# Writing the layer norms' row-wise products and sums on GpSimd as four instructions of 256 columns

## The reference

```
mask = adjacency_matrix.astype(float32) + eye(n) > 0
for l in range(3):
    si = x @ attn_w[l, :d];  sj = x @ attn_w[l, d:]
    scores = leaky_relu(si[:, :, None] + sj[:, None, :] + attn_b[l], 0.2)
    attn = softmax(where(mask, scores, -inf))
    h = layernorm(x + attn @ x, g1[l], beta1[l])
    x = layernorm(h + gelu(h @ W1[l] + b1[l]) @ W2[l] + b2[l], g2[l], beta2[l])
# layernorm(x, gamma, beta) = (x - mu) * rsqrt(var + eps) * gamma + beta
```

## Time and profile before

| | us |
|---|---|
| median of 3 runs | 1895.09 |
| lowest, highest | 1894.74, 1895.41 |
| profiled execution, span | 1892.0 |
| PE busy | 1672.9 (88%) |
| DVE busy | 1513.0 (80%) |
| POOL busy | 1314.4 (69%) |
| ACT busy | 1120.7 (59%) |

### The profile page before, as it was taken

One profiled execution on the slowest core, in us unless ns is written; L12 is line 12 of the kernel. 1 busy time (PEld: TensorE's weight loads), 2 busy tenths in 40 slices (PEclk: granted clock), 3 DMA queues, 4 the chain that ended last, 5 costly groups with the idle time before them and its releaser, 6 DMA issues.

```text
span 1892.0 us, 40139 instructions
## 1 busy us (share of the span) xinstructions
PE 1672.9 (88%) x12032; PEld 1482.6 (78%) x12032; DVE 1513.0 (80%) x5366; ACT 1120.7 (59%) x2718; POOL 1314.4 (69%) x1690
## 2 busy tenths in 40 slices
PE   5999999965999999999899999999989898989895
PEld 4777777754888888888788888888878787878784
DVE  3888888877788778788887887887888888888873
ACT  3888888864556556556465565565554545554542
POOL 3355555534787787787777877877868787888786
PEclk8999999996999999999899999999999898999998
DMA  5233333323121121121211211211212122212101
GB/s 181 63 89 89 89 89 89 89 79 123 34 67 58 42 67 58 42 67 54 91 56 44 67 52 47 67 53 47 67 34 68 64 70 65 68 64 69 63 26 45
DMA packets 150477, 127.31 MB, mean 67 GB/s; under 512 B 14880, under 2 KB 143392, under 8 KB 150432
## 3 DMA queue, kind: packets, MB, share of 16 engines
q1 hardware_dynamic: 145024, 124.30, 21.4%
q10 hardware_dynamic: 5408, 2.50, 0.5%
HBM read 89.03 MB, written 37.75 MB: 67 GB/s over the span
## 4 chain that ended last, share of the span: by engine, by line
PE 24%; DVE 20%; POOL 19%; issue 11%; ACT 3%; POOLq 1%; DVEq 0%; ACTq 0%
PE ps L45 14%; PE ps L819 6%; POOL gnn_norm L154 5%; DVE gnn_junk L913 5%; PE ps L795 3%; DVE gnn_small L929 2%; POOL gnn_norm L742 2%; POOL gnn_h L746 2%; POOL xo L761 2%; POOL gnn_norm L757 2%; POOL inv L149 2%; DVE gnn_small L934 2%; DVE gnn_small L937 2%; DVE gnn_res L972 1%; DVE gnn_st L976 1%
## 5 line engine op out<-in xcount | busy, mean ns | idle before, releaser
L819 PE MATMUL ps<-gnn_w_hi,gnn_g_hi 128*128 128x256 f32 x1536 | 454.8, 296 | 41.7 <-DVE gnn_res L972 41.0
L819 PE MATMUL ps<-gnn_w_lo,gnn_g_hi 128*128 128x256 f32 x1536 | 445.7, 290 | 0.0
L819 PE MATMUL ps<-gnn_w_hi,gnn_g_lo 128*128 128x256 f32 x1536 | 444.9, 290 | 0.0
L141 POOL TENSOR_TENSOR fence_pool<-half_neg 128x1 f32<-128x1 f32 x304 | 64.1, 213 | 477.3 <-DVE gnn_mv L1063 169.0
L980 DVE TENSOR_TENSOR gnn_g_lo<-ps,gnn_g_hi 128x512 fp32r<-128x512 f32 x384 | 263.1, 685 | 135.3 <-ACT ps L893 135.2
L892 ACT ACTIVATE gnn_g_hi<-ps,b_cols 128x512 fp32r<-128x512 f32 x384 | 264.5, 689 | 179.4 <-PE ps L45 155.3
L819 PEld LDWEIGHTS ps<-gnn_w_hi,gnn_g_hi 128*128 128x128 f32 x1536 | 305.6, 199 | 47.5 <-DVE gnn_res L972 44.8
L45 PE MATMUL ps<-gnn_hT_hi,gnn_w_hi 128*128 128x512 f32 x768 | 333.4, 434 | 4.0 <-DVE gnn_g_lo L980 4.0
L869 ACT ACTIVATE gnn_e<-gnn_u,gnn_small 128x128 f32<-128x128 f32 x192 | 74.9, 390 | 400.3 <-DVE gnn_small L938 400.3
L819 PEld LDWEIGHTS ps<-gnn_w_lo,gnn_g_hi 128*128 128x128 f32 x1536 | 306.7, 200 | 1.9
L819 PEld LDWEIGHTS ps<-gnn_w_hi,gnn_g_lo 128*128 128x128 f32 x1536 | 305.8, 199 | 0.0
(11 more groups left out here) (116 smaller groups left out, 3925.2 us busy)
## 6 DMA issues: line engine op xcount, KB each, us to landing
hist<-xo SPq DMA_DIRECT2D x48, 512.0 KB, 3.3
x<-hist SPq DMA_DIRECT2D x48, 512.0 KB, 4.3
gmask<-mask_hist SPq DMA_DIRECT2D x48, 256.0 KB, 4.5
aw<-in_L_gnn_attn_w SPq DMA_DIRECT2D x48, 256.0 KB, 4.3
att_xq<-in_x SPq DMA_DIRECT2D x16, 512.0 KB, 4.8
att_xl<-in_x SPq DMA_DIRECT2D x16, 512.0 KB, 3.5
gnn_fin<-hist SPq DMA_DIRECT2D x16, 512.0 KB, 3.8
out<-gnn_fin SPq DMA_DIRECT2D x16, 512.0 KB, 2.8
```

Source lines behind the costliest of these rows:

```text
L141: e.tensor_tensor(fence_pool[:, n:n + 1], half_neg[:, 0:1], half_neg[:, 0:1], ALU.add)
L819: mm = e.matmul(FF2[j % 2], g[a][:, m, j * N:(j + 1) * N], V[b][:, m, :], start=(n == 0), stop=(n == len(terms) - 1))
```

## The change

Each of the five instructions of 128x1024 becomes four of 128x256, one for each graph; `row` gives one row and no longer repeats it. The semaphore is raised by the last of the four. Nothing else is written differently: waits, values and the order on all engines stay.

```
                 def row(l, n):
-                    return affine[:, bass.ds(l, 1), n, :].to_broadcast([P, GROUP, D])
+                    return affine[:, bass.ds(l, 1), n, :].rearrange("p o d -> p (o d)")
...
                     e.wait_ge(ln1, 6 * t1 + 5)
-                    e.tensor_tensor(norm[:], norm[:], row(l, 0), ALU.mult).then_inc(ln1, 1)
+                    for j in range(GROUP):
+                        ins = e.tensor_tensor(norm[:, j, :], norm[:, j, :], row(l, 0), ALU.mult)
+                    ins.then_inc(ln1, 1)
...
-                    e.tensor_tensor(h[:], norm[:], row(l, 1), ALU.add).then_inc(h_out, 1)
-
-                    e.tensor_tensor(hb[par1][:], norm[:], row(l, 2), ALU.add).then_inc(hb_out, 1)
+                    for j in range(GROUP):
+                        ins = e.tensor_tensor(h[:, j, :], norm[:, j, :], row(l, 1), ALU.add)
+                    ins.then_inc(h_out, 1)
+
+                    for j in range(GROUP):
+                        ins = e.tensor_tensor(hb[par1][:, j, :], norm[:, j, :], row(l, 2), ALU.add)
+                    ins.then_inc(hb_out, 1)
...
-                    e.tensor_tensor(norm[:], norm[:], row(l, 3), ALU.mult).then_inc(ln2, 1)
+                    for j in range(GROUP):
+                        ins = e.tensor_tensor(norm[:, j, :], norm[:, j, :], row(l, 3), ALU.mult)
+                    ins.then_inc(ln2, 1)
...
-                    e.tensor_tensor(xo[par][:], norm[:], row(l, 4), ALU.add).then_inc(x_out, 1)
+                    for j in range(GROUP):
+                        ins = e.tensor_tensor(xo[par][:, j, :], norm[:, j, :], row(l, 4), ALU.add)
+                    ins.then_inc(x_out, 1)
```

## The result

| | before | changed |
|---|---|---|
| median | 1894.57 us | 1899.27 us |
| lowest, highest (9 runs each) | 1892.05, 1895.41 | 1896.46, 1903.24 |
| profiled execution, span | 1892.0 | 1897.3 |
| POOL busy | 1314.4 | 1438.7 |

A forecast was written before the change was run, and what follows sets the result against it. POOL was taken to bound the first two layers. Steady steps +5, PE's clock +31, last layer +4, start and end +2.5 on 1892.0 gave 1934.5; with 3.1 for the median of the runs, 1937, range 1894 to 1966.

The forecast's parts named there:

- rival (1): PE's clock holds: then +11.5, 1907 us; chance 0.20, range 1895 to 1912.
- The signs named for being right: Groups 2.75 to 2.85; L939, L947 under 0.8; behind h 5.5 to 6 or 7 to 7.5; PE's stall 2 to 2.5.
- The ring and its bound: First two layers: POOL sets the 28.33 us steady step, 21.16 of it on POOL and 7.17 behind h.
- Four quarters: Each group of four costs POOL +0.40 us over one instruction; four groups count in a steady step, +1.60.
- rival (2): Quarters cost next to nothing, at most 0.1 to 0.2 a group: 1860 us; chance 0.12.
- What DVE gets back: Behind h, DVE's small instructions wait less: 7.17 becomes 5.59, -1.58 a step; their slipping between quarters adds +0.15.
- PE's clock: A 2.3 us stall before the transposes lowers the clock in 0.6 of 30 steps, 1.7 each: +31 us.
- PEclk at 9 in all slices: Sign of being wrong: granted PE clock at 9 in all the page's slices of the first two layers.
- The last layer: POOL never idle, a step of 31.85 for 31.52: +0.3 a step over 14 steps, +4 us.
- Start and end: The first and last norms run alone, six groups: +2.5 us.
- Rival (3): `probs_max` gets in before h's last quarter, holds POOL 0.66, clock always falls: +76, 1975 us; chance 0.10.
- Rival (4): DVE gains nothing, the 7.17 behind h stays: +53 to +60, 1955 us; chance 0.10.

The follow-up runs named there:

- the PSUM kernel: Kernel before, no group cut, rows of DVE's small tile placed in PSUM so its small instructions read at most one SBUF tensor: 1803.05 us, ratio 0.9523.
- keeping PE busy: Changed kernel plus twelve unused transposes of the identity on PE ahead of its wait for h: 1874.39 us, ratio 0.9909.
- three groups cut: Kernel before with only the three groups of `ln_attention` (product, h, hb) in quarters, `ln_ffn` whole: 1855.84 us, ratio 0.9803.
- changed, small rows in PSUM: Changed kernel, all five groups in quarters, with the rows of DVE's small tile in PSUM: 1932.75 us, ratio 1.0202.

## Why the prediction was right and wrong

The forecast was +42 and the measurement is +4.7. The step that failed is the account of POOL's and DVE's standing still for each other. The sum took DVE's small instructions as a cost to POOL (+0.15 a step) and put at nothing, without a reason, what POOL gets back in its own fronts; the runs showed 0.2 to 0.9 a step less there, so that the ring without a fall of the clock became shorter, and the last layer gained 9.5 us where +4 was forecast. The second step is one of size: 31 for the falls of the clock, of which some 22 came. The measured 1899 lies inside the stated range, but in the interval of rival (1), 1895 to 1912, whose mechanism, that the clock holds, did not happen: that number would be right by luck. The signs named for being right came in the steady steps: groups of 2.78 to 2.83, L939 at 0.80 and L947 at 0.16, stretches of 5.58 and 7.07, stalls of 1.94 and 2.27.

**The ring and its bound** were read rightly. POOL sets a steady step, the ends of L929 and L937 with POOL's instructions were the sign of DVE standing still, and the PSUM kernel shows it directly.

**Four quarters** cost +0.40 in the forecast by the line between two sizes; measured 2.83 for 2.40, +0.43. Right, and so falls rival (2).

**What DVE gets back**: 7.17 to 5.59 was forecast, 5.58 measured. Right. The +0.15 beside it, for small instructions slipping in between POOL's quarters, had the wrong sign: the groups bear it already, and the front of `ln_attention` is shorter, by 0.31 in one body of the loop (fence to product 5.78 for 6.09) and by 0.10 in the other. The parts that shrank are POOL's small instructions: L149 takes 1.03 for 1.19 and L151 0.26 for 0.45. They stand beside DVE's `attention_sums`; that this is the cause was not tested. Over a ring POOL's part grew by about 1.4, not 1.75. So without the fall of the clock a step is 28.25 on average (28.42 and 28.08), 0.2 shorter than before, where I had forecast 0.17 longer; over 30 steps that is 10 us of the error.

**PE's clock**: the mechanism was right and two things in its price were off. PE's stall ahead of h is 1.94 or 2.27 (forecast 2.3), and none is left at the next `probs_T`. The clock fell in 13 of the 28 steady steps, where I had put 0.6, and again at both changes of layer; and a fall costs 1.49 on the ring (7.07 less 5.58), not 1.7. With the 15 long stretches that makes 22 for 31 forecast; keeping PE busy gained 24, some 2 of them by other means.
The granted clock over the 4 us from the start of the transposes, in the steady steps of the first two layers of six kernels, goes with the stalls like this:

| kernel | stalls in turn | steps at 1.00 |
|---|---|---|
| before | 1.14 | all |
| changed, PE kept busy | 0.55, 0.88 | all |
| three groups cut | 1.44, 1.75 | all |
| `ln_ffn` alone cut | 1.53, 1.79 | all |
| changed | 1.94, 2.27 | 15 of 28 |
| changed, small rows in PSUM | 2.38, 2.72 | 8 of 28 |

The others of the last two kernels read 0.57 to 0.67. So the longer stall brings the fall more often, but it doesn't decide a single step: in the changed kernel the same 1.94 stands at 1.00 in one layer and at 0.66 in the other. My interpolation from two stalls came near the rate (0.6 for 0.46), with some luck, since the stall alone does not give it; what sets the turn stays open. The Trainium skill, page "TensorE: Matmul & The Clock Gate", section "Part 1: The HAM clock gate", by which I had considered that a short wait does nothing, would have given no fall; the stretches with 0.66 behind 1.94 and 0.57 behind 2.27 speak against taking it so here. I had named PEclk at 9 in all slices of these layers as a sign that I was wrong. That was a bad sign to name: a fall of a few microseconds in every second step leaves most slices at 9.

**The last layer** failed in its sign: +0.3 a step forecast, -0.8 measured, which is 14 us of the error. The mechanism was seen (POOL's 3.5 of idle gone, L992 and L943 among the quarters), but the step of 31.85 was put together from bounds. `final_sum` (now L1002) costs POOL 0.87 where I took all of its 1.2; `probs_max` costs 0.44 and not 0.66, since a part of each lies in POOL's own gaps; and from the final norm's fence to that of `ln_ffn`, and from the fence of `ln_attention` to its product, POOL takes 4.61 and 5.52 where it took 4.97 and 6.09. Together 0.33 + 0.22 + 0.36 + 0.57 = 1.5, less the 0.15 (5 x 0.03) by which the groups are longer: 1.3, which is about the error in this step (31.85 for 30.60); its neighbours take 30.94, and over the layer the error is 1.1 (31.85 for 30.77). I had added what DVE would take from POOL, and nothing for what DVE, standing still less, no longer takes.

**Start and end** were right within a microsecond: +2.72 and -0.42 for +2.5.

So of the 37 us by which the forecast was too high, some 10 come from the ring, 14 from the last layer, 9 from the price and rate of the clock, and 4 from the layer changes and the rest, which I have not taken apart. The omission, with the +0.15 that had the wrong sign, makes all of the first and about two thirds of the second, some 19; the prices of `final_sum` and `probs_max` make the remaining third. Rival (3) did not happen in the steady steps, but `probs_max` comes up at 1035.60 and h's last quarter of 0.72 begins at about 1035.1, so by an estimate half a microsecond less would bring it; and at each of the two changes of layer it did happen: `probs_max` and the casts of the next layer's weights fell among h's quarters, h took 4.20, PE's stall was 3.35, and the clock read 0.57 and 0.58. Rival (4) falls by the 5.58.

## What to carry to other kernels

A VectorE instruction that ends within some hundredths of a microsecond with a GpSimd instruction, and takes far longer than its shape needs, is a sign of waiting for it. See first whether an operand can be put in PSUM (here 4.8%, for 28 us more of GpSimd's busy time); cutting a GpSimd instruction in four makes it 18% longer, and is worth it only where something urgent stands still beside it (product and h of `ln_attention` alone: 2.4%). Sum both directions, what the freed engine takes from the other and what it no longer takes, and ask whether PE's idle pieces gather into one: two of 1.1 and 1.0 did no harm here, one of some 2 cost 1.5 us in about every second step.

## What the hardware showed beyond this

A GpSimd product of 128x256 takes 0.74 us and one of 128x1024 2.40; cutting one into two costs 0.13, into four 0.43, so about 0.14 for each instruction more. I had not expected how evenly this goes, nor that DVE's `probs_max` (0.69 alone) beside a whole `hb` would be 0.78 or 2.70 according to which of the two began first. Nor that one addition of 128x4 with an operand moved to PSUM would run in 0.15 in the middle of a GpSimd instruction. And I had not expected that the clock would fall in strict alternation, behind the shorter stall in one layer and behind the longer in the other.
